# Rank counts of the second batch moved from VectorE to GpSimd and TensorE in a one-core kernel with a selective scan

## What is computed

```python
keep_fraction = sigmoid(logits @ score_w + score_b)
rows_to_keep = clip((keep_fraction * total_row_count).astype(int32), 1, None)
row_magnitudes = norm(weight_params, axis=-1)
thresholds = take_along_axis(sort(row_magnitudes)[..., ::-1], (rows_to_keep - 1)[:, None], axis=-1)
return weight_params * (row_magnitudes >= thresholds)[..., None]
```

```python
scores = where(mask, scores, neg)
```

## Time and profile before

| | us |
|---|---|
| median of three timed runs | 560.53 |
| lowest, highest | 555.91, 567.94 |
| the profiled execution | 556.44 |
| its span on the core | 554.6 |

### The profile page before, as it was taken

The page is one execution under the profiler, slowest core; times in us unless marked ns, Lnnn a source line. Parts: engine busy times, 40 slices in busy tenths (PEclk is TensorE's granted clock), DMA queues, the critical chain, the costliest instruction groups (busy, mean ns, idle before and its releaser), DMA issues.

```text
span 554.6 us, 7884 instructions
## 1 busy us (share of the span) xinstructions
PE 462.9 (83%) x2753; PEld 332.0 (60%) x2753; DVE 458.0 (83%) x529; ACT 381.1 (69%) x664; POOL 379.3 (68%) x229
## 2 busy tenths in 40 slices
PE   8968898768858998898679998886997958899992
PEld 6423765445547665765576557554896746777651
DVE  3879799998999799779997997899999989932412
ACT  3675687679977787868877978798668778701210
POOL 5029867866999688839995897599889969500001
PEclk9987899978999999989999999899999979999897
DMA  8330111110001111110121111100111490047004
GB/s 285 124 118 38 39 38 39 38 43 38 32 28 55 40 40 38 41 38 5 36 77 39 38 40 40 40 27 32 56 40 38 189 385 7 1 156 290 1 1 157
DMA packets 17920, 38.88 MB, mean 70 GB/s; under 512 B 1666, under 2 KB 10498, under 8 KB 17875
## 3 DMA queue, kind: packets, MB, share of 16 engines
q1 hardware_dynamic: 17874, 38.32, 19.4%
HBM read 36.08 MB, written 2.23 MB: 69 GB/s over the span
## 4 chain that ended last, share of the span: by engine, by line
PE 41%; DVE 30%; issue 14%; ACT 10%; POOL 3%; DVEq 0%; POOLq 0%; ACTq 0%
DVE scanmem L1779 19%; PE hT L871 8%; DVE yTd L1790 6%; PE pp L567 5%; PE pp L660 4%; PE yacc L631 3%; PE dA L833 2%; ACT dA L1302 2%; PE pp L609 2%; POOL scanmem L1458 2%; PE yacc L627 1%; DVE yTd L1704 1%; PE pp L623 1%; ACT hc L1312 1%; PE pp L732 1%
## 5 line engine op out<-in xcount | busy, mean ns | idle before, releaser
L1458 POOL TENSOR_TENSOR scanmem<-par,scanmem 128x1024 f32<-128x1024 f32 x128 | 300.3, 2368 | 80.4 <-PE hT L871 61.0
L871 PE MATMUL hT<-con,scanmem 128*128 128x128 f32 x1024 | 161.0, 287 | 63.2 <-DVE yTd L1790 42.9
L1302 ACT ACTIVATE dA<-par,Aneg 128x512 f32<-128x512 f32 x256 | 172.0, 690 | 44.4 <-DVE scanmem L1779 42.8
L871 PEld LDWEIGHTS hT<-con,scanmem 128*128 128x128 f32 x1024 | 118.7, 146 | 119.2 <-DVE yTd L1790 39.9
L1779 DVE TENSOR_TENSOR_SCAN scanmem<-dA,carry,scanmem 128x512 f32<-128x512 f32 x128 | 156.2, 1264 | 9.7 <-ACT dA L1302 8.4
L1779 DVE TENSOR_TENSOR_SCAN scanmem<-dA,scanmem 128x512 f32<-128x512 f32 x128 | 148.8, 1204 | 10.2 <-ACT dA L1302 8.4
L1312 ACT ACTIVATE hc<-hT,CTs 128x512 f32<-128x512 f32 x128 | 86.8, 678 | 31.1 <-PE hT L871 31.0
L631 PE MATMUL yacc<-con,hc 128*128 128x128 f32 x512 | 82.1, 286 | 0.3 <-ACT hc L1312 0.3
L1790 DVE SCALAR_TENSOR_TENSOR yTd<-hT,CTs,yTd 128x512 f32<-128x512 f32 x91 | 66.1, 726 | 10.2 <-PE hT L871 10.0
L631 PEld LDWEIGHTS yacc<-con,hc 128*128 128x128 f32 x512 | 64.8, 150 | 0.6 <-ACT hc L1312 0.6
L567 PE MATMUL pp<-xnT,wi 128*128 128x512 f32 x120 | 59.1, 621 | 2.5 <-ACT xnT L1075 1.3
(11 more groups left out here) (199 smaller groups left out, 522.4 us busy)
## 6 DMA issues: line engine op xcount, KB each, us to landing
scanmem<-brow SPq DMA_DIRECT2D x32, 512.0 KB, 3.5
par<-in SPq DMA_DIRECT2D x1, 4096.0 KB, 17.4
scanmem<-in SPq DMA_DIRECT2D x1, 4096.0 KB, 14.7
xt<-in SPq DMA_DIRECT2D x4, 512.0 KB, 6.8
wi<-in SPq DMA_DIRECT2D x2, 1024.0 KB, 7.8
out<-par SPq DMA_DIRECT2D x4, 512.0 KB, 4.1
aw<-in SPq DMA_DIRECT2D x5, 256.0 KB, 6.4
xr<-in SPq DMA_DIRECT2D x1, 1024.0 KB, 9.9
```

The source lines that it names most:

```text
L871: last = nc.tensor.transpose(hT[:, i % 2, m * P:(m + 1) * P], hb[:, n % RING, m, i * P:(i + 1) * P], ident)
L1302: A(dA[:, m % 2, :], delta(c)[:, m, :], ACT.Exp, scale=Aneg[:, m * NS + s:m * NS + s + 1]).then_inc(da_ready, 1)
L1458: nc.gpsimd.tensor_tensor(hb[:, n % RING, ms, :], dx(c)[:, ms, :], Bb[:, row:row + 1, :].to_broadcast([P, 2, T]), ALU.mult).then_inc(bx_re ...
```

## The change

The counts of the second batch are cut into two pieces of work. GpSimd compares the row of norms with one group's norms and writes ones and zeros of 128x1024 (`compare`), in steps 3, 5, 7 (two each), 9 and 12 (one each), ahead of that step's products. TensorE sums them over the partitions with a column of ones: four jobs K, each for two compares, at half-steps 17, 18, 20 and 23 of chunk 0. VectorE copies or adds the 128x8 results half a step later. `kept` comes at the end of step 12, the mask row's load in the second chunk, ahead of the load of its fourth piece of B rows, and its conversion at the end of step 18. The compares are written into tiles that are not in use then.

```diff
+COUNT_AT = [17, 18, 20, 23]
+COMPARE_AT = {3: (0, 1), 5: (2, 3), 7: (4, 5), 9: (6,), 12: (7,)}
+RANKED_AT, MASK_AT = 12, NS + 2
...
+            for j, h in enumerate(COUNT_AT):
+                beside[h] += [("K", 0, j)]
...
+        above = [par[1][:, a, i * S:(i + 1) * S] for a in (3, 2) for i in range(2)] + [junk, x1T[:, 1, :], negm[:, :], par[1][:, 3, 0:S]]
...
-            sp.dma_start(mrow, mask[0:1, :].to_broadcast([P, S])).then_inc(s_mrow, 16)
...
+                    if piece == PIECES + BSLOTS:
+                        sp.wait_ge(ranked, 3)
+                        sp.dma_start(mrow, mask[0:1, :].to_broadcast([P, S])).then_inc(s_mrow, 16)
...
+            def job_K(job, o):
+
+                j = job[2]
+                pe.wait_ge(compared, 2 * (j + 1))
+                for g in range(GB):
+                    for i in range(2):
+                        last = mm(o[:, g:g + 1], above[2 * j + i][:, g * P:(g + 1) * P], ones[:, :], start=i == 0, stop=i == 1)
+                return last
...
+            nc.gpsimd.memset(ones[:, :], 1.0)
...
+            def compare(i):
+
+                if i == 0:
+                    pool.wait_ge(ss_act, 12)
+                    pool.wait_ge(mag_act, 2)
+                if i == 1:
+                    wait_full(pool, ("TP", 0, 0))
+                if i == 4:
+                    pool.wait_ge(scan_done, CT)
+                if i == GB - 1:
+                    wait_full(pool, ("K", 0, 0))
+                g = GB + i
+                nc.gpsimd.tensor_scalar(above[i], magrow, ss[:, g:g + 1], 1.0, ALU.is_lt, ALU.mult).then_inc(compared, 1)
...
+                    for i in COMPARE_AT.get(n, ()):
+                        compare(i)
...
+            def ev_K(job, o):
+                gs = slice(GB, 2 * GB)
+                if job[2] == 0:
+                    last = V.tensor_copy(cnt[:, gs], o[:, 0:GB])
+                else:
+                    wait_read(dve, ("K", 0, job[2] - 1))
+                    last = V.tensor_tensor(cnt[:, gs], cnt[:, gs], o[:, 0:GB], ALU.add)
+                return last
...
-            def batch1_rows(s):
-
-                if s == 0:
-                    dve.wait_ge(s_mrow, 16)
-                    V.tensor_scalar(negm[:, :], mrow, -1.0, FLT_MAX, ALU.add, ALU.mult)
-                    dve.wait_ge(ss_act, 12)
-                    dve.wait_ge(mag_act, 2)
-                if s < GB:
-                    own.after()
-                    own.mark(count(GB + s, magrow, junk))
-                if s == GB:
-                    dve.wait_ge(rstd_ready, 2)
-                    own.after()
-                    kept(slice(GB, 2 * GB), 1)
+            def score_mask():
+
+                dve.wait_ge(s_mrow, 16)
+                V.tensor_scalar(negm[:, :], mrow, -1.0, FLT_MAX, ALU.add, ALU.mult)
+
+            def batch1_rows():
+
+                dve.wait_ge(rstd_ready, 2)
+                wait_read(dve, ("K", 0, GB // 2 - 1))
+                kept(slice(GB, 2 * GB), 1)
...
-                    if c == 0:
-                        batch1_rows(s)
+                    if n == RANKED_AT:
+                        batch1_rows()
+                    if n == MASK_AT:
+                        score_mask()
```

More of the change, by code:

```diff
@@ L248, in build @@
         eps = sb("eps", [P, 1])
+        ones = sb("ones", [P, 1])
         half_b = sb("half_b", [P, CT])
@@ L371, in build @@
         dx_ready = sem("dx_ready")
-        ss_dve, ss_act, mag_pe, mag_act, ranked = sem("ss_dve"), sem("ss_act"), sem("mag_pe"), sem("mag_act"), sem("ranked")
+        ss_dve, ss_act, mag_pe, mag_act, compared, ranked = sem("ss_dve"), sem("ss_act"), sem("mag_pe"), sem("mag_act"), sem("compared"), sem("ranked")
         aexp_ready, A_ready, rstd_ready, fe_ready, init_done = (sem(x) for x in ("aexp_ready", "A_ready", "rstd_ready", "fe_ready", "init_done"))
@@ L824, in job_FB @@
                 return mm(o[:, 0:DM], sel_batch[:, job[1]:job[1] + 1].to_broadcast([P, P]), row3, start=True, stop=True)
-            jobs = dict(F=job_F, TP=job_TP, U=job_U, T=job_T, I=job_I, Z=job_Z, V=job_V, X=job_X, XT=job_XT, D=job_D, Y=job_Y,
+            jobs = dict(K=job_K, F=job_F, TP=job_TP, U=job_U, T=job_T, I=job_I, Z=job_Z, V=job_V, X=job_X, XT=job_XT, D=job_D, Y=job_Y,
                         O=job_O, R=job_R, A=job_A, G=job_G, GT=job_GT, M=job_M, RR=job_RR, S0=job_S0, S1=job_S1, PT=job_PT, YV=job_YV, YT=job_YT,
@@ L1678, in ev_FL @@
                 return V.tensor_copy(flag_i[:, :], flag[0:1, 1:2])
-            evs = dict(F=ev_F, TP=ev_TP, V=ev_V, D=ev_D, G=ev_G, Z=ev_Z, Y=ev_Y, O=ev_O, M=ev_M, S0=ev_S0, S1=ev_S1, VV=ev_VV, W12=ev_W12, H=ev_H, WT=ev_WT, W3=ev_W3, FB=ev_FB, FL=ev_FL)
+            def ev_K(job, o):
[6 more added lines that the diff above has]
+                return last
+            evs = dict(K=ev_K, F=ev_F, TP=ev_TP, V=ev_V, D=ev_D, G=ev_G, Z=ev_Z, Y=ev_Y, O=ev_O, M=ev_M, S0=ev_S0, S1=ev_S1, VV=ev_VV, W12=ev_W12, H=ev_H, WT=ev_WT, W3=ev_W3, FB=ev_FB, FL=ev_FL)
             def read(job):
```

## The result

The changed kernel takes 597.65 us in the median of its four runs (590.19 to 603.67) where the kernel before takes 564.24 beside it. The ratio is 1.0587, with a 95% interval of 1.0389 to 1.0786. The prediction was 560.3 us and a time within 2% of before. In the experiments a time is the median of all of a kernel's runs, and the ratio, with its interval, is to the kernel before beside it.

What follows compares the result with a forecast made beforehand. VectorE was taken as the bound in steps 3 to 8 and 12 to 16 of the first chunk. -3.2 + 2.0 + 2.7 + 0.3 = +1.8 on 556.44 gave 558.2, with run spread 560.3 us; range 553.5 to 567.5.

Steps and rivals of the forecast that it cites:

- Steps 3 to 8 (-4.6): First chunk, steps 3 to 8: without VectorE's counts they take 32.18 us instead of 36.76, a gain of 4.6 us.
- The third chunk: Stage of the earlier trace without counts, used as model: 32.18 us for steps 3 to 8, 33.06 for 8 to 12.
- I take 1.1: Price in us of one GpSimd compare of 128x1024, read from a one-input row of 1.04; free up to 1.28.
- the compares are dear: Rival, chance 0.19: compares above 1.28 us make the X job wait for GpSimd; 565.6 us, or 567.5 at 2.37 each.
- 104.5: Time in us by which TensorE's X job, at step 8 of the first chunk, needs GpSimd's last convolution.
- I take 3.4 us: TensorE's price for one K job of 16 one-column matmuls (32 records); 6.8 at the lower clock level.
- K0 +2.0: K0 at half-step 17: 1.4 of its 3.4 us go into TensorE gaps, 2.0 us push everything behind it.
- in the shape of the O jobs: K1 and K2 at half-steps 18 and 20: already priced in the -3.2 us by the third chunk's O jobs, 3.62 us each.
- The keep factors (+2.7): Three small VectorE instructions, now behind step 12, wait for GpSimd with nothing hiding them: 2.7 us, bounds 0.5 and 4.9.
- K3 at 0: K3 at half-step 23, ahead of steps 12 to 16 where TensorE idles 6.3 us: no cost, bounds 0 and 2.0.
- The sum, +1.8: Net of all terms for the whole kernel: -3.2 + 2.0 + 2.7 + 0.3 = +1.8 us.
- dear compares with K jobs at the low clock: Combined case for a result slower by over 2%: +9.0 and 3.4 us more; chance of slower 0.05.

Runs made afterwards that it cites:

- experiment 2: Kernel before plus seven GpSimd one-input instructions of 128x1024 in the head, to price compare, multiply, subtract, max and min forms; one run, 557.74 us.
- experiment 1: Changed kernel with GpSimd multiplying where it compared, counts left out, K jobs still of one column; 573.64 us, 1.0334 of the kernel before.
- experiment 5: Experiment 1 with the K jobs streaming 64 columns of ones instead of one, same matmuls and weights; 562.41 us, 1.0086 of the kernel before.
- experiment 7: Kernel before with only the three keep-factor instructions moved from behind step 8 to behind step 12; 568.94 us, 1.0135.
- the tenth: Kernel before plus two useless TensorE jobs of eight 128-column matmuls at half-steps 17 and 18; 557.57 us, 1.001.
- the ninth: Kernel before with counts moved to other VectorE places, plus two useless TensorE jobs of eight 128-column matmuls; 557.01 us, 0.9978.

## Why the prediction was wrong, and where it was right

**Steps 3 to 8 (-4.6): right.** Forecast 32.18 us, measured 32.58 in the changed kernel and 32.19 and 32.18 where the compares are cheap. The third chunk was a good stand-in.

**"I take 1.1 (bounds 1.04 and the 2.35 of a product; nothing suggests less)": the first step that failed.** A compare takes 3.73 us, outside the bounds. I took the one row of this shape as the price of the form, one input and two scalars, and a product with two inputs as the dearest that an instruction of this size could be; experiment 2 shows that the price goes by the operation, and that the row, two multiplies, is one of the cheap ones. The rival "the compares are dear" had the right mechanism and the right point from which it decides: with its own formula, 57.0 + 7 x 3.73 + 1.41 + 7 x 4.68 + 3.96 = 121.2 us for the last convolution's end, 16.7 late against its 104.5. Measured: 119.3, and 17.0 us of loss by the rows of experiment 1. Only its price stopped at 2.37, and so my range.
The Trainium skill, page "GPSIMD Engine Reference", section "Performance pitfalls for Q7 kernels", gave an estimate of 0.9 to 1.7 us, and section "Engine selection" of the same page says that an elementwise operation with one input goes at about line rate. The runs agree for the multiply (1.12 and 1.17 us) and not for the compare, nor for subtract, max and min; the measurement decides.

**"A K job ... I take 3.4 us", K0 +2.0, K1 and K2 "in the shape of the O jobs": the second step that failed.** 3.4 was right for the job at the upper level (3.63 in experiment 1). I held the low level for a bound on one job's price, 6.8, and never asked which level the jobs themselves would leave behind. They ran at 6.83, and the transposes and D jobs behind them at half speed, +11.7 us in steps 9 to 12 (38.56 us in experiment 1; 35.14 - 8.31 = 26.83 in experiment 5, where step 8 to 9 is also 8.31). The O job of the earlier trace rows, by which K1 and K2 were priced, streams 256 columns, and the rows that I had for few columns were too short to show it. With 64 columns the forecast holds: 33.06 + 2.0 = 35.06 us for steps 8 to 12, measured 35.14 in experiment 5.

**The keep factors (+2.7): right,** 2.63 us up to the next scan in the changed kernel, and 2.61 in experiment 5. My upper bound of 4.9 was met too, by the 5.0 of experiment 7. In all these rows the ones that wait end some hundredths of a microsecond behind GpSimd's instruction. The Trainium skill's page "SBUF — State Buffer", section "SBUF: two separate sides", describes, for some forms of VectorE's instructions, an exclusive lock on the port pair that the two engines share, held for a whole instruction; the rows agree with such a lock in every case that I read.

**K3 at 0: too low.** In experiment 5 step 12 to 13 takes 9.75 us where it takes 5.72 before; the keep factors are 2.61 of the difference of 4.0, and 0.95 us is a wait for ScalarE, so K3 is about 1.4. In the changed kernel the step takes 11.82 us, 2.1 more, at the lower clock that K3's one-column matmuls have behind them, as K1's do.

**The sum, +1.8.** Where both failed steps are taken away, step 13 comes at 148.19 us against 145.39, so +2.8, and the whole is 1.0086 times the kernel before, some 4.8 us. The other 2 us appear in the second chunk: from the start of GpSimd's 39th product to that of its 43rd it is 12.97 us in the kernel before, 15.13 in experiment 5, and 15.46 in experiment 2, which changes nothing there. So they seem to belong to the run and not to the change; I didn't separate them.

**The chances.** I gave 0.05 to the case that came, "dear compares with K jobs at the low clock", and priced it at +9.0 and 3.4 more. Both of its parts happened, and each was larger than I had it: 14 to 17 us, and 11 to 15. The range ended at 567.5 us because it held only one of them, and that at too low a price.

## What to carry to other kernels

In this kernel an instruction's price on GpSimd belonged to its operation: before work is moved there, look for a row with that very operation, and where there is none let the upper bound go well beyond the rows of other operations. For matmuls with very few columns ask, beside their own time, what the clock is behind them; their busy time in the profile didn't tell it here, and streaming more columns, which cost next to nothing (3.63 and 3.68 us a job), was the cheaper form. And a term read from another stage of the same trace (here the third chunk) held to a few tenths, where a term read from a similar instruction did not.

## What the runs showed of the hardware

- On a tile of 128x1024 GpSimd's instruction with one input takes 1.04 to 1.17 us with two multiplies, 2.97 for a compare alone, 3.63 to 3.74 for compare and multiply, 3.79 for subtract and multiply, 4.11 for subtract and max, and 4.10 for multiply and min. Add and multiply takes 0.62 on 128x512.
- Matmuls of 128x128 by one column, busy without a pause in the records, were followed by a granted clock at the lower of its two levels (0.50 from 115 to 135 us in the first experiment), and the same number by 64 columns was not (1.00 from 105 to 130 us in the fifth). Behind 128 columns it was 1.00 from 115 to 120 us in the tenth; in the ninth it fell later, to 0.50 from 120 us, without a matmul of one column. At the upper level few and many columns cost nearly the same: 3.63 us for 32 records of one column, 3.68 for 32 of 64 columns.
- Such a stretch lasted: in the first experiment the clock was at 0.50 to 0.56 from 115 to 140 us, with TensorE busy for 5.00 of every 5.00 us, through transposes and D jobs that run at 1.00 in the fifth up to 130 us. K2, of one column too, lies in it. What ends such a stretch isn't shown.
